# Batch 7's experts in the turned form, pair (1,0) second in the load queue, bias columns computed earlier

## The chip, the cores and the metric

The kernel runs on one core of one Trainium2 chip. The metric is the device time of one execution in microseconds, lower is better. A core has TensorE (matrix products, into PSUM banks), VectorE, ScalarE and GpSimd (elementwise work), SyncE (here it only issues transfers) and 16 DMA engines.

## The reference, cut to what matters

Eight batches of 128 rows by 128 channels, float32, pass through four residual layers. Layers 0 and 1 are mixed linear layers; the third is a mixture of experts with two chosen experts for each batch and one shared expert; the fourth picks one expert for each batch.

```python
# third layer (S=128, H=128, I=512, E=8, two experts of 8 for each batch)
w, sel = jax.lax.top_k(softmax(router_logits), 2)
w = w / w.sum(axis=-1, keepdims=True)
out  = sum over the two experts e of batch b:  w[b, e] * mlp(x[b], gate[e], up[e], down[e])
out += mlp(x, shared_gate, shared_up, shared_down)
# mlp(x, g, u, d) = (gelu(x @ g) * (x @ u)) @ d
# fourth layer (H=256, one expert of 8 for each batch)
up, gate = x @ W_up[e].T + b_up[e], x @ W_gate[e].T + b_gate[e]
out = (silu(up) * gate) @ W_down[e].T + b_down[e]
```

## The kernel before, in words

Everything is unrolled and ordered by hand: each engine has its own written list of steps, and semaphores tie them together. A step that waits holds up all that stands behind it on its engine.

**Stages.** Layers 0 and 1 are done by about 14 us. The shared expert follows, in eight steps `k` (four chunks of 128 for each half of the batches): TensorE forms gate and up in three wide products each (`shared_high`, `shared_middle`, `shared_low`; a float32 factor is split in a rounded part and a rest), ScalarE takes the gelu (L413) and rounds the hidden tile (`round_hidden`, L469), VectorE multiplies (`hidden`, L665), GpSimd subtracts the rounded part (`hidden_low_part`, L362), and `shared_down(k)` takes both. Then come the chosen experts, pair `(b, k)` being expert `k` of batch `b`, and layer 3 of batch `b` (called layer 3 in the code, the fourth of the reference) once both pairs are summed.

**Plain and turned batches.** In a plain batch (0 and 7) `gate_up` multiplies each 128-column chunk of a weight with x, in plain float32: 8 matmuls, 16 records of 128 columns in the trace. Its hidden tile has the hidden index on the partitions, and `down` (L935) reads it directly. In a turned batch (1 to 6) `gate_up_wide` makes x the stationary factor and streams 512 columns of weights: 3 products for gate and 3 for up (L918, L919, L921). For them ScalarE rounds both weights (`round_part`, L451, a ring of four in `wide_h`) and GpSimd forms the rests (`wide_low_part`, L357). The hidden tile comes out the other way round, so VectorE transposes it in 32 x 32 blocks (`turn`, L681) and SyncE swaps the blocks' places with four transfers of 128 KB (`swap`, L255), each 128 pieces of 1 KB; `down` then waits for `swapped`.

**Loads.** SyncE issues all of them, in an order written out: 16 pairs of 768 KB, 8 weights of layer 3 of 384 KB (`load_w3`), the swaps and the stores. There are 11 places for pairs, so the loads from (5,1) on wait until an earlier pair's down product is complete; those of (4,0) to (5,0) wait for the last `shared_down` (`down_done`, 8). `swap(b)` waits for both transposes of batch b and, from batch 3 on, for the down products of batch b - 2, whose tile it overwrites.

**Orders that matter here.** ScalarE, in the shared expert: gelu(k), round_hidden(k - 1), and from k = 4 one `round_part` of batch 1. SyncE: pairs (0,0), (0,1), (1,0), the weights of layer 3 of batch 0, (1,1), (2,0) and on. VectorE: the experts' selected biases (`bias_columns`: a product over 320 elements, a sum, a halving) between batch 1 and layer 3 of batch 0; ScalarE's `halve3` waits for them. `layer3(b)` on TensorE is four products into PSUM (L950), `down3(b)` its last two (L965).

Of the kernel before, what the change touches and what calls it, by code (L numbers as in the profile page):

```python
# [5 lines left out]
B, S, C = 8, 128, 128  # L6
E = 8
# [4 lines left out]
HC = H // 128  # L12
# [8 lines left out]
NSH = 2 * T  # L21
# [5 lines left out]
TURNED = range(1, B - 1)  # L27
# [9 lines left out]
def build(nc, x, head, rest_in, shared, skill, layer3, out):  # L37
# [8 lines left out]
    with ctx:  # L46
# [183 lines left out]
        with nc.Block() as block:  # L230

            @block.sync
            def _(sp):
# [37 lines left out]
                def pick(b, k):  # L271
                    picked[b, k] = expert(b, k)

                def load(b, k):
                    load_pair(b, k, picked[b, k])
# [3 lines left out]
                pick(0, 1)  # L279
                load(0, 1)  # L280
                pick(1, 0)
                load(1, 0)
                load_w3(0, picked[0, 0])
                for b, k in ((1, 1), (2, 0), (2, 1), (3, 0)):
                    pick(b, k)
                    load(b, k)
# [35 lines left out]
                for b in range(2, B - 2):  # L322
                    store(b, b % 2)
# [4 lines left out]
            def _(pool):  # L328
# [36 lines left out]
                for k in range(4):  # L365
                    hidden_low_part(k)
                wide_low_part(1, 0, 0)
                hidden_low_part(4)
                wide_low_part(1, 0, 1)
                hidden_low_part(5)  # L370
                wide_low_part(1, 1, 0)
                hidden_low_part(6)
                hidden_low_part(7)
                wide_low_part(1, 1, 1)
# [6 lines left out]
            def _(act):  # L381
# [90 lines left out]
                for k in range(1, NSH):  # L472
                    gelu_step(k, k % 2, shg_ps[k % 3])
                    round_hidden(k - 1)
                    if k >= 4:
                        round_part(1, (k - 4) // 2, (k - 4) % 2)
                round_hidden(NSH - 1)
                gelus(0)
# [13 lines left out]
                for b in range(5, B):  # L492
                    gelus(b)
                    if b == 5:
                        round_pair(6, 1)
                    halve3(b - 3)
                    tanh_step(b - 3)
                halve3(B - 3)
# [8 lines left out]
            def _(dve):  # L507
# [139 lines left out]

                def bias_columns():

                    n = 2 * HC + 1  # L650
                    then(dve.tensor_tensor(bias_hot[:, :, :, :], bias_t.unsqueeze(2).broadcast_to([128, n, B, E]),
                                           hot1[:, :, :].unsqueeze(1).broadcast_to([128, n, B, E]), ALU.mult))
                    then(dve.reduce_sum(bsel[:, :, :], bias_hot[:, :, :, :], axis=AX.X))
                    dve.tensor_scalar(half_bias[:, :, :], bsel[:, 0:HC, :], 0.5, None, ALU.mult).then_inc(bias_ready, 1)
# [96 lines left out]
                second_share()  # L751
                hidden(3, 1)
                share_sum()
                hidden(4, 0)
                share_scale()
                hidden(5, 1)
# [8 lines left out]
                add_shared(0)  # L765
                expert_hidden(1, 0)
                add_shared(1)
                residual(0)
                expert_hidden(1, 1)
                bias_columns()  # L770
# [29 lines left out]
            def _(pe):  # L800
# [214 lines left out]
                for b in range(5, B - 1):  # L1015
                    gate_up_wide(b, 0)
                    gate_up_wide(b, 1)
                    down3(b - 4, b % 2)
                    down(b - 2, 0)
                    down(b - 2, 1)  # L1020
                    layer3(b - 3)
                gate_up(B - 1, 0)
                gate_up(B - 1, 1)
                down3(B - 5, 1)
                down(B - 3, 0)
                down(B - 3, 1)
                layer3(B - 4)
                down(B - 2, 0)
                layer3(B - 3)
                down(B - 2, 1)  # L1030
                down3(B - 4, 0)
                down(B - 1, 0)
                down3(B - 3, 1)
                product3(B - 2, 0, 0, 0)
# [60 lines left out]
```

## Time and profile before

| | |
|---|---|
| median of 3 runs | 87.89 us (86.85 to 87.95) |
| the profiled execution, its own time | 86.78 us |
| its span, first to last instruction | 85.4 us |
| TensorE, matmuls | 78.1 us busy (91%) |
| VectorE; ScalarE; GpSimd | 52.3; 47.1; 46.0 us busy |
| transfers | 21.65 MB; the main queue 69.4% of 16 engines' span |
| granted TensorE clock | 1.0 throughout |

The busy times are averages over stages with different limits; the stages have to be read one by one. The span leaves out what lies before the first and behind the last instruction, 1.4 us of this execution.

### The profile page before, as it was taken

The page shows a single profiled execution, that of the slowest core. Times are in us where ns is not written, and L with a number is a line of the kernel's source. Part 1 is how long each engine was busy: PE and PEld are TensorE (multiplying, and loading weights), DVE is VectorE, ACT ScalarE, POOL GpSimd, SP SyncE. Part 2 cuts the span into 40 slices and gives each one's busy share as a digit, 9 for nine tenths or more (in the row PEclk, how much of TensorE's full clock was granted, in tenths as well). Part 3 has the DMA queues.
Part 4 walks back from the last instruction along what each step waited for, and adds up shares of the span by engine and source line. Part 5 has one row for each costly group of instructions (what it writes and reads, how often), then busy time and mean ns, then how long its engine had stood idle before and what let it go on. Part 6 is the DMA issues. An engine that isn't in the chain of part 4 may idle for free.

```text
span 85.4 us, 1612 instructions
## 1 busy us (share of the span) xinstructions
PE 78.1 (91%) x500; PEld 68.4 (80%) x500; DVE 52.3 (61%) x116; ACT 47.1 (55%) x95; POOL 46.0 (54%) x44
## 2 busy tenths in 40 slices
PE   6999899999994889999947999999999999999990
PEld 6979788888862778896825897988986999999990
DVE  1599399884003454449969983959645944456271
ACT  6500996864069859507489695572292072059270
POOL 3020567589129999999998999992092000000000
PEclk9999999999999999999999999999999999999999
DMA  1996000789999999389977999989999988600102
GB/s 15 380 373 239 3 0 0 236 348 365 405 397 423 426 407 394 125 282 374 421 203 140 345 376 291 321 222 319 352 402 396 370 247 189 222 0 8 37 24 61
DMA packets 8791, 21.65 MB, mean 253 GB/s; under 512 B 976, under 2 KB 5200, under 8 KB 8784
## 3 DMA queue, kind: packets, MB, share of 16 engines
q1 hardware_dynamic: 8496, 20.77, 69.4%
q10 hardware_dynamic: 288, 0.79, 2.4%
q8 instruction: 4, 0.07, 0.3%
q14 instruction: 3, 0.02, 0.1%
HBM read 17.88 MB, written 0.52 MB: 216 GB/s over the span
## 4 chain that ended last, share of the span: by engine, by line
PE 43%; DMA 27%; POOL 7%; DVE 7%; SPq 6%; ACT 4%; issue 4%; DVEq 0%
PE bank L935 15%; DMA pair_w<-in_skill 9%; DMA b_mix<-p 8%; PE bank L908 7%; DMA shared_sb<-in_shared 6%; PE bank L950 5%; PE bank L918 4%; PE bank L965 3%; PE bank L919 3%; PE bank L921 3%; POOL pair_low L357 3%; SPq L255 3%; POOL hid_l L362 3%; DMA head_sb<-in_head 3%; SPq L240 2%
## 5 line engine op out<-in xcount | busy, mean ns | idle before, releaser
L357 POOL TENSOR_TENSOR pair_low<-pair_w,wide_h 128x512 fp32r<-128x512 f32 x16 | 20.5, 1307 | 7.5 <-ACT wide_h L451 7.3
L413 ACT ACTIVATE gelu<-bank 128x512 f32<-128x512 f32 x24 | 14.0, 593 | 9.2 <-PE bank L921 6.5
L667 DVE SCALAR_TENSOR_TENSOR hid<-gelu,wsel,bank 128x512 f32<-128x512 f32 x16 | 11.8, 736 | 6.8 <-PE bank L935 2.2
L451 ACT ACTIVATE wide_h<-pair_w 128x512 fp32r<-128x512 f32 x16 | 9.3, 622 | 6.5 <-DMA pair_w<-in_skill 6.4
L918 PE MATMUL bank<-wide_h,x_h 128*128 128x512 f32 x24 | 10.0, 418 | 1.8 <-DVE hid L667 1.8
L362 POOL TENSOR_TENSOR hid_l<-hid,hid_h 128x512 fp32r<-128x512 f32 x8 | 10.2, 1288 | 1.9 <-ACT hid_h L469 1.9
L665 DVE TENSOR_TENSOR hid<-gelu,bank 128x512 f32<-128x512 f32 x8 | 5.5, 687 | 8.7 <-ACT gelu L413 4.4
L681 DVE STREAM_TRANSPOSE p<-hid 128x512 f32<-128x512 f32 x12 | 8.5, 712 | 1.7 <-DMA b_mix<-p 1.4
L919 PE MATMUL bank<-wide_h,x_l 128*128 128x512 f32 x24 | 9.4, 390 | 0.0
L423 ACT ACTIVATE half<-bank,half_bias 128x128 f32<-128x128 f32 x12 | 3.7, 361 | 10.0 <-PE bank L950 7.1
L908 PE MATMUL bank<-x_t,pair_w 128*128 128x128 f32 x64 | 7.8, 278 | 0.7 <-DVE hid L665 0.7
L908 PEld LDWEIGHTS bank<-x_t,pair_w 128*128 128x128 f32 x64 | 7.4, 192 | 1.2 <-DVE hid L665 1.2
L918 PEld LDWEIGHTS bank<-wide_h,x_h 128*128 128x128 f32 x24 | 4.5, 189 | 2.9 <-DVE hid L667 2.2
L712 DVE SCALAR_TENSOR_TENSOR gate<-bank,bsel,half 128x128 f32<-128x128 f32 x12 | 3.7, 346 | 5.1 <-ACT half L423 5.1
L950 PE MATMUL bank<-x_t,w 128*128 128x128 f32 x48 | 6.4, 277 | 0.2 <-DVE x_t L688 0.2
L921 PE MATMUL bank<-pair_low,x_h 128*128 128x512 f32 x16 | 6.4, 398 | 0.0
L341 POOL TENSOR_TENSOR shared_l<-shared_sb,shared_h 128x512 fp32r<-128x512 f32 x3 | 3.9, 1288 | 4.6 <-ACT shared_h L391 4.5
L950 PEld LDWEIGHTS bank<-x_t,w 128*128 128x128 f32 x48 | 5.8, 192 | 0.6 <-DVE x_t L688 0.6
L469 ACT ACTIVATE hid_h<-hid 128x512 fp32r<-128x512 f32 x8 | 5.0, 628 | 2.1 <-DVE hid L665 2.0
L871 PE MATMUL bank<-x_h,shared_h 128*128 128x512 f32 x16 | 5.8, 395 | 0.0
L879 PE MATMUL bank<-x_h,shared_l 128*128 128x512 f32 x16 | 5.8, 390 | 0.0
L919 PEld LDWEIGHTS bank<-wide_h,x_l 128*128 128x128 f32 x24 | 4.5, 189 | 0.7
(114 smaller groups left out, 157.1 us busy)
## 6 DMA issues: line engine op xcount, KB each, us to landing
pair_w<-in_skill SPq DMA_DIRECT2D x12, 768.0 KB, 8.0
w<-in_layer SPq DMA_DIRECT2D x6, 384.0 KB, 8.3
x_t<-p SPq DMA_DIRECT2D x12, 128.0 KB, 3.5
b_mix<-p SPq DMA_DIRECT2D x12, 128.0 KB, 4.0
shared_sb<-in_skill SPq DMA_DIRECT2D x1, 768.0 KB, 12.3
home_h<-in_skill SPq DMA_DIRECT2D x1, 768.0 KB, 4.6
home_l<-in_skill SPq DMA_DIRECT2D x1, 768.0 KB, 6.1
home_hid<-in_skill SPq DMA_DIRECT2D x1, 768.0 KB, 7.6
```

The lines of the kernel that those rows point to most:

```text
L357: pool.tensor_tensor(low_of(b, k)[:, m, :], w[:, m, :], wide_h[:, ring_at(b, k) % RING, m, :].bitcast(fp32), ALU.subtract).then_inc(wide_l ...
L362: pool.tensor_tensor(hid_l[:, k % 3, :], hid[:, k % 2, :], hid_h[:, k % 3, :].bitcast(fp32), ALU.subtract).then_inc(hid_low, 1)
L413: act.activation(gelu[:, n, :], ps[:, :], ACT.Gelu_apprx_tanh).then_inc(gelu_ready, 1)
L451: act.activation(wide_h[:, ring_at(b, k) % RING, m, :], w[:, m, :], ACT.Copy).then_inc(wide_high, 1)
L667: dve.scalar_tensor_tensor(hid[:, n, :], gelu[:, n, :], wsel[:, bass.DynSlice(weight, 1)], u_ps[n][:, :], ALU.mult, ALU.mult).then_inc(hid ...
L681: dve.transpose(turned[q][:, :, k, :], hid[:, k, :].rearrange("p (j s) -> p j s", j=T)).then_inc(turned_ready, 1)
L908: mm = pe.matmul(ps[:, S * t:S * (t + 1)], w[:, 1 + n, 128 * t:128 * (t + 1)], x2_t[:, columns(b)], start=True, stop=True)
L918: pe.matmul(ps[:, :], x2_h[:, S * b:S * (b + 1)], wide_h[:, n % RING, m, :], start=True, stop=False)
L919: pe.matmul(ps[:, :], x2_l[:, S * b:S * (b + 1)], wide_h[:, n % RING, m, :], start=False, stop=False)
L921: pe.matmul(ps[:, :], x2_h[:, S * b:S * (b + 1)], low_of(b, k)[:, m, :], start=False, stop=True).then_inc(done, 1)
L935: mm = pe.matmul(acc_ps(b)[:, 0:S].rearrange("p (a s) -> p a s", s=QUAD), w[:, part, C * t:C * (t + 1)], by_chunk[:, t, :, :], start=(k == ...
L950: pe.matmul(ps[:, S * c:S * (c + 1)], w[:, n, 128 * c:128 * (c + 1)], x3_t[:, b % 4, :], start=True, stop=True).then_inc(done, 1)
```

## The change

Batch 7 joins the turned batches (`TURNED`). With it come its four roundings on ScalarE (the pair (7,0) after batch 5's layer-3 step, (7,1) after batch 6's gelus), four subtractions on GpSimd, two transposes on VectorE, and `swap(7)` on SyncE, for which `store(2, 0)` is moved ahead. On TensorE the order of the end is changed: both down steps of batch 6 come before layer 3 of batch 5, and the first product of batch 6's layer 3 comes ahead of batch 7's first down step.

At the start, SyncE loads (1,0) second, then (0,1), (1,1), and only then the first weights of layer 3. ScalarE rounds (1,0) one step k later, and (1,1) between the two gelus of batch 0; GpSimd's subtractions follow that order. The bias columns are split in three steps, spread between the shared expert's hidden products on VectorE, and the second add of the shared sum comes ahead of the product of (1,0).

```diff
--- before.py
+++ after.py
@@ -24,7 +24,7 @@
 PAIRS, THIRD = 7, 3
 RING = 4
 IN_BANK = 4
-TURNED = range(1, B - 1)
+TURNED = range(1, B)
 
 
 HEAD = 2 * C + B + B * E
@@ -276,12 +276,11 @@
 
                 pick(0, 0)
                 load(0, 0)
-                pick(0, 1)
-                load(0, 1)
-                pick(1, 0)
-                load(1, 0)
+                for b, k in ((1, 0), (0, 1), (1, 1)):
+                    pick(b, k)
+                    load(b, k)
                 load_w3(0, picked[0, 0])
-                for b, k in ((1, 1), (2, 0), (2, 1), (3, 0)):
+                for b, k in ((2, 0), (2, 1), (3, 0)):
                     pick(b, k)
                     load(b, k)
                 pick(3, 1)
@@ -319,7 +318,9 @@
                 store(1, 1)
                 swap(6)
                 load_w3(7, picked[7, 0], 3)
-                for b in range(2, B - 2):
+                store(2, 0)
+                swap(7)
+                for b in range(3, B - 2):
                     store(b, b % 2)
                 store(B - 2, 0)
                 store(B - 1, 1)
@@ -362,15 +363,14 @@
                     pool.tensor_tensor(hid_l[:, k % 3, :], hid[:, k % 2, :], hid_h[:, k % 3, :].bitcast(fp32),
                                        ALU.subtract).then_inc(hid_low, 1)
 
-                for k in range(4):
+                for k in range(5):
                     hidden_low_part(k)
                 wide_low_part(1, 0, 0)
-                hidden_low_part(4)
+                hidden_low_part(5)
                 wide_low_part(1, 0, 1)
-                hidden_low_part(5)
-                wide_low_part(1, 1, 0)
                 hidden_low_part(6)
                 hidden_low_part(7)
+                wide_low_part(1, 1, 0)
                 wide_low_part(1, 1, 1)
                 for b in TURNED[1:]:
                     for k in range(TOP_K):
@@ -472,10 +472,12 @@
                 for k in range(1, NSH):
                     gelu_step(k, k % 2, shg_ps[k % 3])
                     round_hidden(k - 1)
-                    if k >= 4:
-                        round_part(1, (k - 4) // 2, (k - 4) % 2)
+                    if k in (5, 6):
+                        round_part(1, 0, k - 5)
                 round_hidden(NSH - 1)
-                gelus(0)
+                gelu_step(NSH, 0, g_ps[0])
+                round_pair(1, 1)
+                gelu_step(NSH + 1, 1, g_ps[1])
                 round_batch(2)
                 gelus(1)
                 round_batch(3)
@@ -491,10 +493,12 @@
                 tanh_step(1)
                 for b in range(5, B):
                     gelus(b)
-                    if b == 5:
-                        round_pair(6, 1)
+                    if b < B - 1:
+                        round_pair(b + 1, 1)
                     halve3(b - 3)
                     tanh_step(b - 3)
+                    if b == 5:
+                        round_pair(7, 0)
                 halve3(B - 3)
                 tanh_step(B - 3)
                 act.preload_act_table(ACT.Silu)
@@ -645,12 +649,17 @@
                     mark(dve.scalar_tensor_tensor(wsel[:, :].rearrange("p (b k) -> p b k", k=TOP_K), wnorm[:, :, :],
                                                   STOP_SCALE, wpart[:, :, :], ALU.mult, ALU.add))
 
+                def bias_pick():
+                    n = 2 * HC + 1
+                    mark(dve.tensor_tensor(bias_hot[:, :, :, :], bias_t.unsqueeze(2).broadcast_to([128, n, B, E]),
+                                           hot1[:, :, :].unsqueeze(1).broadcast_to([128, n, B, E]), ALU.mult))
+
                 def bias_columns():
-
-                    n = 2 * HC + 1
-                    then(dve.tensor_tensor(bias_hot[:, :, :, :], bias_t.unsqueeze(2).broadcast_to([128, n, B, E]),
-                                           hot1[:, :, :].unsqueeze(1).broadcast_to([128, n, B, E]), ALU.mult))
-                    then(dve.reduce_sum(bsel[:, :, :], bias_hot[:, :, :, :], axis=AX.X))
+                    settled()
+                    mark(dve.reduce_sum(bsel[:, :, :], bias_hot[:, :, :, :], axis=AX.X))
+
+                def bias_halves():
+                    settled()
                     dve.tensor_scalar(half_bias[:, :, :], bsel[:, 0:HC, :], 0.5, None, ALU.mult).then_inc(bias_ready, 1)
 
                 def hidden(k, n, weight=None):
@@ -749,10 +758,13 @@
                 first_share()
                 hidden(2, 0)
                 second_share()
+                bias_pick()
                 hidden(3, 1)
                 share_sum()
+                bias_columns()
                 hidden(4, 0)
                 share_scale()
+                bias_halves()
                 hidden(5, 1)
                 norm_shares()
                 hidden(6, 0)
@@ -763,11 +775,10 @@
                 expert_hidden(0, 0)
                 expert_hidden(0, 1)
                 add_shared(0)
+                add_shared(1)
                 expert_hidden(1, 0)
-                add_shared(1)
                 residual(0)
                 expert_hidden(1, 1)
-                bias_columns()
                 layer3(0)
                 expert_hidden(2, 0)
                 expert_hidden(2, 1)
@@ -1012,26 +1023,20 @@
                 down(2, 0)
                 down(2, 1)
                 layer3(1)
-                for b in range(5, B - 1):
+                for b in range(5, B):
                     gate_up_wide(b, 0)
                     gate_up_wide(b, 1)
                     down3(b - 4, b % 2)
                     down(b - 2, 0)
                     down(b - 2, 1)
                     layer3(b - 3)
-                gate_up(B - 1, 0)
-                gate_up(B - 1, 1)
-                down3(B - 5, 1)
-                down(B - 3, 0)
-                down(B - 3, 1)
-                layer3(B - 4)
                 down(B - 2, 0)
+                down(B - 2, 1)
                 layer3(B - 3)
-                down(B - 2, 1)
                 down3(B - 4, 0)
+                product3(B - 2, 0, 0, 0)
                 down(B - 1, 0)
                 down3(B - 3, 1)
-                product3(B - 2, 0, 0, 0)
                 down(B - 1, 1)
                 pe.wait_ge(silu3_ready, 1)
                 product3(B - 2, 0, 0, 1)
```

## Rows read from the trace of the kernel before

**Rows 1.** Chain of work that ended last, shares of the span by engine
```profile
PE 43%; DMA 27%; POOL 7%; DVE 7%; SPq 6%; ACT 4%; issue 4%; DVEq 0%
```

**Rows 2.** Timeline, ScalarE: start, length, instruction, count, [idle before <-releaser]
```profile
19.62 0.62 ACT L469 ACTIVATE hid_h<-hid 128x512 fp32r<-128x512 f32 x1
...
24.34 0.63 ACT L451 ACTIVATE wide_h<-pair_w 128x512 fp32r<-128x512 f32 x1 [4.09 <-DMA pair_w<-in_skill]
```

**Rows 3.** Loads by time of issue (15.3; 16.4): size, us to landing
```profile
pair_w<-in_skill SPq DMA_DIRECT2D x1, 768.0 KB, 7.1
...
pair_w<-in_skill SPq DMA_DIRECT2D x1, 768.0 KB, 7.9
```

**Rows 4.** Timeline of GpSimd
```profile
25.05 1.28 POOL L357 TENSOR_TENSOR pair_low<-pair_w,wide_h 128x512 fp32r<-128x512 f32 x1 [3.44 <-ACT wide_h L451]
...
33.68 9.21 POOL L357 TENSOR_TENSOR pair_low<-pair_w,wide_h 128x512 fp32r<-128x512 f32 x7
...
62.02 2.54 POOL L357 TENSOR_TENSOR pair_low<-pair_w,wide_h 128x512 fp32r<-128x512 f32 x2 [3.89 <-ACT wide_h L451]
```

**Rows 5.** Timeline of TensorE, first half
```profile
20.74 0.62 PE L887 MATMUL bank<-x_l,shared_h 128*128 128x512 f32 x2
...
34.86 0.39 PE L918 MATMUL bank<-wide_h,x_h 128*128 128x512 f32 x1
...
36.22 1.95 PE L935 MATMUL bank<-hid,pair_w 128*128 128x128 f32 x16
...
45.46 0.50 PE L918 MATMUL bank<-wide_h,x_h 128*128 128x512 f32 x1 [1.79 <-DVE hid L667]
```

**Rows 6.** Timeline of VectorE around the bias columns
```profile
41.05 0.69 DVE L651 TENSOR_TENSOR bias_hot<-rest_sb,hot 128x320 f32<-128x320 f32 x1
...
42.30 0.63 DVE L654 TENSOR_SCALAR half_bias<-bsel 128x16 f32<-128x16 f32 x1
...
44.67 0.74 DVE L667 SCALAR_TENSOR_TENSOR hid<-gelu,wsel,bank 128x512 f32<-128x512 f32 x1
```

**Rows 7.** Stretches: engines' busy time, granted clock, DMA share, GB/s
```profile
34.00:37.00 3.00, 3.00 (x19) 2.60 (x17) 1.21 (x2) 1.37 (x3) 3.00 (x3) 1.00 0.51 137
43.00:46.00 3.00, 1.21 (x5) 0.69 (x5) 2.25 (x5) 2.97 (x8) 2.76 (x3) 1.00 0.64 154
47.50:54.40 6.90, 6.90 (x44) 5.92 (x43) 5.12 (x10) 5.02 (x10) 6.90 (x7) 1.00 0.99 342
```

**Rows 8.** VectorE's wait; loads issued 54.4, 55.6, 59.5; batch 4's swap, 58.0
```profile
65.74 0.71 DVE L681 STREAM_TRANSPOSE p<-hid 128x512 f32<-128x512 f32 x1 [0.95 <-DMA b_mix<-p]
...
pair_w<-in_skill SPq DMA_DIRECT2D x1, 768.0 KB, 6.9
...
pair_w<-in_skill SPq DMA_DIRECT2D x1, 768.0 KB, 8.6
...
pair_w<-in_skill SPq DMA_DIRECT2D x1, 768.0 KB, 8.1
...
b_mix<-p SPq DMA_DIRECT2D x2, 128.0 KB, 6.5
```

**Rows 9.** The end: TensorE, VectorE, SyncE; landing of batch 6's swap
```profile
68.47 3.74 PE L908 MATMUL bank<-x_t,pair_w 128*128 128x128 f32 x32
72.05 0.61 PE L965 MATMUL bank<-hid,late_w 128*128 128x128 f32 x4
...
76.07 1.06 PE L950 MATMUL bank<-x_t,w 128*128 128x128 f32 x8
...
79.64 0.39 PE L950 MATMUL bank<-x_t,w 128*128 128x128 f32 x2
...
78.05 0.29 DVE L688 TENSOR_TENSOR x_t<-bank,x2s 128x128 f32<-128x128 f32 x1
...
67.86 3.03 SPq L255 DMA_DIRECT2D b_mix<-p  x4
...
b_mix<-p SPq DMA_DIRECT2D x1, 128.0 KB, 3.0
```


## The prediction

> **What bounds the kernel now.** I read the chain that ended last first [rows 1]: TensorE (PE) holds 43% of it and transfers 27%, so two things are nearly full at once. The timelines then say where. PE works back to back from 45.5 us on, and its idle time lies before that, behind one late transfer. ScalarE finishes a rounding at 20.25 us and next has the rounding of the first turned pair, (1,0), in its order; that pair lands at 24.3, so the engine stands still for 4.09 us with five gelus and roundings of the shared layer queued behind [rows 2]. The load table shows why: the pair is third in SyncE's queue. The second transfer, issued at 15.3 and 7.1 us on its way, lands at 22.4; the third, issued at 16.4, takes 7.9 and lands at 24.3 [rows 3]. GpSimd (POOL) idles 3.44 us, from 21.6 to 25.05 [rows 4], and then runs on without a pause: 25.05 to 33.68 is seven subtractions, 1.23 us each. PE reaches the first wide products at 34.86 instead of running through [rows 5]. A second stall is at 45.46, 1.79 us, released by the hidden product of VectorE (DVE) for pair (2,0); that product stands behind the bias columns, 41.05 to 42.93, and behind layer 3 of batch 0 [rows 5, 6].
>
> The other resource is the DMA engines. From 47.5 to 54.4 they are busy for 0.99 of the time; only two gaps of size are left after 30 us: 34 to 37 at a share of 0.51 (1.5 us idle) and 43 to 46 at 0.64 (1.1 us idle) [rows 7]. Where PE waits in the second half, it waits for these or comes just behind them: DVE's transpose of (6,0) waits 0.95 us for the swap of batch 4, which lands at 65.7 [rows 8], and POOL idles 3.89 us before the low parts of pair (6,1), whose load took 6.9 us from 54.4 and landed at 61.3 [rows 4, 8].
>
> **First part: the queue at the start.** Pair (1,0) takes the second place and lands near 22.4 instead of 24.3; (0,1) lands at 24.3, and PE wants it near 27.9, so it costs nothing. The rounding of (1,0) also moves behind the next gelu. ACT is free at 20.25; PE's fifth shared product is complete about 21.1 (its last two products start at 20.74 [rows 5]), so the gelu runs 21.2 to 21.8, the rounding of that hidden tile to 22.4, and POOL starts its next subtraction at 22.4. From there to the low part of (1,1), second half, stand eight subtractions: 22.4 + 8 x 1.23 = 32.3, against 33.68 + 1.23 = 34.9 before [rows 4]. PE: from 20.74 there are 2 + 3 + 6 + 3 + 6 + 3 = 23 wide matmuls of 0.228 each (six of them from 34.86 to 36.22 [rows 5]), 5.2 us, then batch 0's plain products, 2 x 1.79, then nine more of 0.228, 2.05: 20.74 + 5.2 + 3.6 + 2.05 = 31.6. I find no wait in between that outlasts this (the last low part of the shared layer is there at 29.9). So (1,0) starts at about 31.7 rather than 34.86: **PE is 3.1 us ahead.**
>
> **Second part: bias columns.** Three DVE instructions leave 41.05 to 42.93 (1.9 us). Their new places lie among the shared hidden products, where DVE waits for gelus and low parts anyway; 0.65, 0.5 and 0.6 us delay three hidden products by 0.3 to 0.6, all of which wait for POOL or ScalarE anyway. Without that cover they would cost at most the same 1.9 us. At the far end: PE could be at pair (3,0) at 31.7 + 1.37 + 1.79 + 1.37 + 0.9 + 2.74 = 39.9. ACT has gelu (1,1) done at 36.5, then four roundings of 0.57, two halves, a tanh: 39.8; DVE gates by 40.4 and forms (2,0) by 41.2. So a stall of 1.3 us stays of the 1.79, and (3,0) starts at 41.2 instead of 45.46: 4.2 us ahead. The second add of the shared sum only trades places with one hidden product, into time where DVE waits for PE's down product; nothing.
>
> A row and a rule on the bias steps: the last of them writes 16 elements a partition and yet takes 0.63 us, ending at 42.93 [rows 6], just as POOL's long group ends at 42.89 [rows 4]. The Trainium skill, page "SBUF — State Buffer", section "SBUF: two separate sides", says that VectorE and GpSimd share a port pair as an exclusive lock held for the whole instruction; the trace agrees in this instruction. By that rule each of the three could be held for a whole subtraction in its new place, and the final gain would be some 0.4 us smaller than my sum. The sum itself takes the rows as they are.
>
> **How much of 4.2 us survives the DMA engines.** They do the same work as before, in nearly the same order, so what they deliver can only come earlier by the idle time that is filled. The loads of batch 4 may go when the shared sum is complete, at 31.8 instead of some 35 [rows 5], which is before the queue runs dry: the gap at 34 to 37 closes, 1.5 us. The next loads stand behind the swap of batch 1, which follows PE's lead of 3 us, so the gap at 43 to 46 closes, 1.1 us. Sum 2.6, and small idle shares elsewhere may add up to 0.4 (a guess). PE was touching the DMA already, so its lead falls to **3.0 us** by batch 6 (2.6 to 3.4): pair (6,1) lands at 58.3 instead of 61.3, the swap of batch 4 near 62.7.
>
> **Third part: batch 7 turned.** Removed: 32 matmul records from 68.47 to 72.05, 3.58 us [rows 9]. Added: 12 wide matmuls of 0.228, 2.74. PE gains **0.84 us**. Beside it: ACT gets four roundings of 0.57 (2.3 us, in a stretch where it has six instructions of its own); POOL four subtractions (5.0 us) where it has ended; DVE two transposes of 0.71 [rows 8]. Are they in time? Pair (7,1) was issued at 59.5 and took 8.1 us, so it landed at 67.6, and the plain products wanted it at 70.3 [rows 8, 9]. Now 64.6, and two roundings of 0.6 and two subtractions come after it; the second subtraction starts 1.25 behind the first: 64.6 + 0.6 + 2 x 1.25 = 67.7. PE, 3.0 ahead, comes to that matmul at 68.0. No stall, 0.3 to spare. The rounding of (7,0) stands in ACT's order ahead of batch 6's gelus; issued at 55.6 and 8.6 us on its way [rows 8], that pair landed at 64.2 and will at 61.2. That delays a gelu by some 2 us and the swap of batch 6 by 1, to 71.2, when PE wants it at 71.3.
>
> **Fourth part: the swap and the end.** Before, DVE's hidden product went straight to PE. Now four more transfers of 128 KB follow, on SyncE behind the swap of batch 6, the last weights and a store, and they also wait for the down product (5,1). PE: wide products of batch 7 end at 68.2, then 0.45 + 1.79 = 70.45. SyncE issues four in 2.6 us or so (3.03 us for batch 6's four), each 3.0 us to land [rows 9]: issue of the last 72.4, landing 75.4. PE meanwhile has layer 3 of batch 4, down (6), layer 3 of batch 5 and a layer-3 down, 0.9 + 1.79 + 0.9 + 0.45 (records of 128 columns follow each other at 3.58 / 32 = 0.112 us; these steps have 8, 16, 8 and 4), and stands at 74.5 before the first product of batch 6's layer 3. That one now stands ahead of down (7,0) and needs the residual of batch 6. The same steps before: layer 3 of batch 5 starts at 76.07, the residual ends at 78.34, 2.27 later [rows 9]. Now 73.15 + 2.3 = 75.5. So PE stalls **1.0 us**, and the swap is hidden under the same stall. Bounds: 0 if both are quicker, 2.5 if SyncE or the landing is 1.5 us slower. From there to the end: before 85.4 - 79.64 = 5.76 with this product in it, now one down step (0.9) and one layer-3 down (0.45) more: 75.5 + 7.1 = 82.6.
>
> **Sum**, against the profiled execution: -3.0 (lead) - 0.84 + 1.0 = -2.8. Span 85.4 to 82.6, its time 86.78 to 84.0. The three runs have a median 1.1 us above that execution and one of them is with it, so I put the new median halfway, at 84.5. About 2% (1.8 us) is what a measurement here tells from nothing.
>
> **Rivals.**
> 1. The DMA engines do not limit (chance 0.2). PE keeps 4.2 ahead: -4.2 - 0.84 + 1.0 = -4.0, profiled 82.8. For it: the packets of swaps keep the engines busy at a low rate, and could run quicker if spread. Against: 0.99 busy for seven us.
> 2. The head start is smaller (0.2). Pair (1,0) lands later than 22.4, or the bias steps hold up the shared layer by one subtraction or more, or ACT's early wait for (7,0) pushes batch 6's swap: lead 2.0, stall 1.2, -1.6, profiled 85.1.
> 3. The start does nothing (0.06): (1,0) still lands at 24.3, or the loads of the next pairs slide by as much. Only the 0.84 and the stall are left: -0.8 to +0.3; profiled 86.5.
> 4. Slower (0.04). One mechanism, the swap of batch 7. From its landing to the end stand down (7,0), a layer-3 down, down (7,1) and 4.65: 6.9 us. It makes the kernel no faster from a landing at 78.5, and slower by 2% from one at 80.2. If its transfers need 6.5 us, as those of batch 4 did behind queued loads [rows 8], and no lead was made (issue from 73.5), it lands at 82.0 and the span is 88.9, +3.5. Against: after 74 us the queue is nearly empty.
> My forecast has 0.5. Range of the median: 83.0 (rival 1, low base) to 86.4 (rival 2, high base). Faster by over 2%: 0.5 + 0.2 + half of rival 2 = 0.79; slower 0.04; the rest 0.17.
>
> **What would show it.** ACT's wait at L451 near 20 us gone or under 0.3 us, POOL continuous from 22.4; first L918 matmul near 31.7; the stall before pair (3,0) about 1.3 us; DMA share over 0.9 throughout 34 to 46; PE waiting for swaps or for low parts between 49 and 62 us, where its lead shrinks from 4 to 3; wide products for batch 7 without a stall; one PE stall of about 1 us at L950 before the last down products, with DVE's L688 as the releaser. The prediction is wrong if PE stays 4 ahead past 60 us, if a stall over 1.5 us stands at the last L935 with a DMA as the releaser, or if the DMA gaps stay open.

## The result, and the profile after

The changed kernel takes 83.47 us (median of 4, 83.01 to 84.70) against 87.37 us (86.62 to 87.95) before: ratio 0.956, 95% interval 0.942 to 0.970, faster. Two later measurements of the same kernel gave 83.73 us each (against 87.30 and 87.31), ratios 0.957 (0.951 to 0.964) and 0.976 (0.968 to 0.983). Every ratio in this document compares only the executions within 1.5% of the fastest of their kernel, so it can differ from the quotient of the medians, which are of all executions. Forecast: 84.5, range 83.0 to 86.4.

The profile taken with the result is of the slowest execution, 84.70 us with a span of 83.0; so where a time matters I also show the last of the later profiles (83.48 us, span 81.9), called the quicker profile below. First the one with the result. ScalarE (ACT), TensorE (PE), GpSimd (POOL), VectorE (DVE) and SyncE, timelines, engine by engine (start, length, instruction, idle time before it and what ended it):

```profile
22.19 0.62 ACT L469 ACTIVATE hid_h<-hid 128x512 fp32r<-128x512 f32 x1
22.71 0.62 ACT L451 ACTIVATE wide_h<-pair_w 128x512 fp32r<-128x512 f32 x1
...
32.11 0.39 PE L929 MATMUL bank<-wide_h,x_h 128*128 128x512 f32 x1
...
41.21 0.50 PE L929 MATMUL bank<-wide_h,x_h 128*128 128x512 f32 x1 [0.79 <-DVE hid L676]
...
51.43 2.05 PE L946 MATMUL bank<-b_mix,pair_w 128*128 128x128 f32 x16 [1.97 <-DMA b_mix<-p]
...
75.83 0.49 PE L961 MATMUL bank<-x_t,w 128*128 128x128 f32 x2 [0.71 <-DVE x_t L697]
...
22.89 1.29 POOL L363 TENSOR_TENSOR hid_l<-hid,hid_h 128x512 fp32r<-128x512 f32 x1 [0.75 <-ACT hid_h L469]
...
21.62 0.55 DVE L663 TENSOR_SCALAR half_bias<-bsel 128x16 f32<-128x16 f32 x1
...
71.18 2.50 SPq L255 DMA_DIRECT2D x_t<-p  x4
```

Batch 7's swap, its last transfer, size and us to landing:

```profile
x_t<-p SPq DMA_DIRECT2D x1, 128.0 KB, 2.8
```

The two stretches in which transfers had idled (the last three columns are granted clock, DMA share and GB/s):

```profile
34.00:37.00 3.00, 3.00 (x23) 2.75 (x22) 1.75 (x4) 0.85 (x2) 3.00 (x4) 1.00 1.02 390
43.00:46.00 3.00, 3.00 (x21) 2.44 (x21) 2.33 (x5) 1.95 (x4) 3.00 (x3) 1.00 0.96 292
```

What is to be seen: the wait of 4.09 us [rows 2] is gone; ACT rounds pair (1,0) with no idle time before it. PE reaches the wide products at 32.1 instead of 34.86 [rows 5], pair (3,0) at 41.2 instead of 45.46. Both DMA gaps [rows 7] are closed, 0.51 to 1.02 and 0.64 to 0.96. And there is a stall that was not there: 1.97 us before down (2,0), released by batch 2's swap. The last stall, 0.71, is the one before batch 6's first layer-3 product.

The three stalls of PE after 28 us in the quicker profile of the changed kernel:

```profile
40.70 0.50 PE L929 MATMUL bank<-wide_h,x_h 128*128 128x512 f32 x1 [0.79 <-DVE hid L676]
...
50.30 2.05 PE L946 MATMUL bank<-b_mix,pair_w 128*128 128x128 f32 x16 [1.36 <-DMA b_mix<-p]
...
74.70 0.49 PE L961 MATMUL bank<-x_t,w 128*128 128x128 f32 x2 [0.71 <-DVE x_t L697]
```

The lead of PE over the kernel before, read from the starts of the same steps in the two timelines (before, and the quicker profile):

| step | before | changed | lead, us |
|---|---|---|---|
| first wide product | 34.86 | 31.60 | 3.26 |
| pair (3,0) | 45.46 | 40.70 | 4.76 |
| down (2,0), behind the stall of 1.36 | 53.36 | 50.30 | 3.06 |
| first product of batch 7 | 68.47 | 64.75 | 3.72 |
| layer-3 down behind batch 7's products | 72.05 | 67.57 | 4.48 |
| last group of matmuls | 82.32 | 78.82 | 3.50 |

The lead grows by 0.66 between 53 and 68 us because two short waits of the kernel before are gone (a low part of pair (6,1) at 64.62, batch 4's swap at 65.69), by 0.76 through batch 7's wide products, and loses 0.98 at the last stall (0.71 idle, the rest its restart). The span is 85.4 - 81.9 = 3.5 shorter.

### The profile page after: what moved, and what is told of

Same layout as the page of the kernel before. It is cut to its first block, busy times and chain, and to the rows that moved or that the text cites. A ratio compares the mean times of both kernels' runs of the same rounds, so it can differ in the third digit from the quotient of the medians.

```text
span 83.0 us, 1591 instructions
## 1 busy us (share of the span) xinstructions
PE 76.8 (93%) x480; PEld 68.1 (82%) x480; DVE 54.2 (65%) x118; ACT 49.4 (59%) x99; POOL 50.7 (61%) x48
## 4 chain that ended last, share of the span: by engine, by line
PE 82%; DMA 7%; DVE 4%; SPq 2%; issue 2%; ACT 1%; DVEq 0%; ACTq 0%
PE bank L946 15%; PE bank L961 8%; DMA b_mix<-p 7%; PE bank L929 6%; PE bank L932 6%; PE bank L930 6%; PE bank L882 4%; PE bank L898 4%; PE bank L890 4%; PE bank L919 4%; PE bank L821 4%; PE bank L813 3%; PE bank L976 3%; SPq L255 2%; PE bank L906 2%; PE bank L908 2%
## 5 line engine op out<-in xcount | busy, mean ns | idle before, releaser
L358 POOL TENSOR_TENSOR pair_low<-pair_w,wide_h 128x512 fp32r<-128x512 f32 x20 | 25.2, 1293 | 4.3 <-ACT wide_h L451 4.3
L451 ACT ACTIVATE wide_h<-pair_w 128x512 fp32r<-128x512 f32 x20 | 11.5, 623 | 4.0 <-DMA pair_w<-in_skill 4.0
L929 PE MATMUL bank<-wide_h,x_h 128*128 128x512 f32 x28 | 11.7, 416 | 0.8 <-DVE hid L676 0.8
L690 DVE STREAM_TRANSPOSE p<-hid 128x512 f32<-128x512 f32 x14 | 10.0, 712 | 2.0 <-DMA b_mix<-p 1.0
L930 PE MATMUL bank<-wide_h,x_l 128*128 128x512 f32 x28 | 10.9, 391 | 0.0
L932 PE MATMUL bank<-pair_low,x_h 128*128 128x512 f32 x20 | 7.8, 390 | 0.0
L929 PEld LDWEIGHTS bank<-wide_h,x_h 128*128 128x128 f32 x28 | 5.3, 189 | 2.0 <-DVE hid L676 1.2
L946 PE MATMUL bank<-x_t,pair_w 128*128 128x128 f32 x48 | 6.3, 277 | 0.0
L946 PEld LDWEIGHTS bank<-x_t,pair_w 128*128 128x128 f32 x48 | 5.8, 192 | 0.4 <-DMA x_t<-p 0.4
L946 PE MATMUL bank<-b_mix,pair_w 128*128 128x128 f32 x32 | 4.0, 278 | 2.0 <-DMA b_mix<-p 2.0
```

The lines of the kernel that those rows point to most:

```text
L358: pool.tensor_tensor(low_of(b, k)[:, m, :], w[:, m, :], wide_h[:, ring_at(b, k) % RING, m, :].bitcast(fp32), ALU.subtract).then_inc(wide_l ...
L451: act.activation(wide_h[:, ring_at(b, k) % RING, m, :], w[:, m, :], ACT.Copy).then_inc(wide_high, 1)
L690: dve.transpose(turned[q][:, :, k, :], hid[:, k, :].rearrange("p (j s) -> p j s", j=T)).then_inc(turned_ready, 1)
L929: pe.matmul(ps[:, :], x2_h[:, S * b:S * (b + 1)], wide_h[:, n % RING, m, :], start=True, stop=False)
L930: pe.matmul(ps[:, :], x2_l[:, S * b:S * (b + 1)], wide_h[:, n % RING, m, :], start=False, stop=False)
L932: pe.matmul(ps[:, :], x2_h[:, S * b:S * (b + 1)], low_of(b, k)[:, m, :], start=False, stop=True).then_inc(done, 1)
```

## The experiments

Each is told against the kernel before, run beside it on the same chip. Three chips were used, four kernels on each; the medians of before were 86.51, 87.30 and 87.31 us.

### The change in parts

**Start only.** The kernel before with the load queue and the new order of roundings and subtractions:

```diff
-                pick(0, 1)
-                load(0, 1)
-                pick(1, 0)
-                load(1, 0)
+                for b, k in ((1, 0), (0, 1), (1, 1)):
+                    pick(b, k)
+                    load(b, k)
                 load_w3(0, picked[0, 0])
...
-                    if k >= 4:
-                        round_part(1, (k - 4) // 2, (k - 4) % 2)
+                    if k in (5, 6):
+                        round_part(1, 0, k - 5)
```

> The kernel before with only the start changed: pair (1,0) second in the load queue and the roundings and subtractions of batch 1 in their new order; bias columns stay between batches 1 and 2, batch 7 stays plain. Theory (the DMA engines cap the lead): PE reaches the first wide products about 3 us earlier, keeps about 2.2 at pair (3,0) because the bias columns still stand in the way there, and ends 1.9 to 2.4 us faster than before. Rival (no cap, PE's own stalls decide): the full 3.0 us, and the DMA share between 34 and 46 us stays well under 0.9.

Measured: 88.82 us (88.19 to 89.34, 4 runs), ratio 1.040 (1.021 to 1.060). Neither theory: **slower than before**, each of its four executions above all seven of before (85.00 to 87.82). The timelines of this kernel, DVE, then POOL, then PE:

```profile
38.08 4.84 DVE L651 TENSOR_TENSOR bias_hot<-rest_sb,hot 128x320 f32<-128x320 f32 x1
42.95 0.49 DVE L653 TENSOR_REDUCE bsel<-bias_hot 128x40 f32<-128x320 f32 x1
43.48 0.17 DVE L654 TENSOR_SCALAR half_bias<-bsel 128x16 f32<-128x16 f32 x1
...
30.10 10.02 POOL L356 TENSOR_TENSOR pair_low<-pair_w,wide_h 128x512 fp32r<-128x512 f32 x8
40.09 2.48 POOL L356 TENSOR_TENSOR shared_low<-shared_sb,wide_h 128x512 fp32r<-128x512 f32 x2
46.32 2.52 POOL L356 TENSOR_TENSOR shared_h<-home_h,wide_h 128x512 fp32r<-128x512 f32 x2 [3.75 <-ACT wide_h L449]
...
46.19 0.79 PE L918 MATMUL bank<-wide_h,x_h 128*128 128x512 f32 x1 [5.53 <-DVE hid L667]
```

Its stretches around the stall:

```profile
40.00:45.00 5.00, 0.66 (x3) 0.19 (x2) 4.19 (x5) 1.28 (x4) 2.57 (x3) 0.87 0.92 264
46.00:50.00 4.00, 3.81 (x11) 3.24 (x12) 2.93 (x5) 2.40 (x5) 3.68 (x3) 0.50 0.44 159
```

The product of the bias columns, 0.69 us before [rows 6], took 4.84 us. It ends at 42.92, and POOL's unbroken run, whose last ten subtractions the first two lines show, ends at 42.57: the product got through only when POOL had nothing left to do. Behind it waits ACT's `halve3`, behind that DVE's hidden product, and PE stood idle for 5.53 us. The granted clock fell from 1.00 to 0.50 (the 1.2 GHz level) between 43 and 44 us, in the middle of that stall, and was full again from 51 us. So the stretch from pair (3,0) to down (1,0) took 51.51 - 46.19 = 5.3 us where the changed kernel needs 44.12 - 40.70 = 3.4: another 1.9 us.

**Bias columns only.**

```diff
                 second_share()
+                bias_pick()
                 hidden(3, 1)
                 share_sum()
+                bias_columns()
                 hidden(4, 0)
                 share_scale()
+                bias_halves()
```

> The kernel before with only the bias columns moved among the shared hidden products (and the second shared add ahead of pair (1,0)). Theory: the stall of 1.79 us before pair (3,0) falls to under 1 us, the DMA gap at 43 to 46 us closes partly while that at 34 to 37 stays; 0.8 to 1.4 us faster. Rival (the three bias steps are held by GpSimd's port lock and slow the shared layer): the first wide product later than 34.9, gain under 0.4 us.

Measured: 86.86 us against 86.51, ratio 1.018 (0.996 to 1.039): no difference that can be told, and my theory's 0.8 to 1.4 us are not there. The rival had the time right and its cause wrong: the first wide product starts at 34.47, not later than 34.9, and the three bias steps take 0.48, 0.49 and 0.55 us in their new places. PE in its profile:

```profile
43.57 0.50 PE L925 MATMUL bank<-wide_h,x_h 128*128 128x512 f32 x1 [0.80 <-DVE hid L672]
53.17 2.05 PE L942 MATMUL bank<-b_mix,pair_w 128*128 128x128 f32 x16 [1.55 <-DMA b_mix<-p]
```

The stall at pair (3,0) fell to 0.80 as expected, and PE was 1.9 us ahead there. All but 0.2 us of it was gone at down (2,0), behind a wait of 1.55 us for batch 2's swap: batch 4's loads had been issued only 0.4 us earlier than before (34.83 against 35.22), and the DMA share from 34 to 37 us was still 0.56.

**Batch 7 only.**

```diff
-TURNED = range(1, B - 1)
+TURNED = range(1, B)
```

with `swap(7)` and the new orders of the end.

> The kernel before with only batch 7 turned and the end's order rearranged. Theory: 0.84 us fewer matmul time, and a stall of 0.7 to 1.0 us before the first layer-3 product of batch 6 (released by VectorE's residual): within 0.4 us of before. Rival (the stall is covered and the turn pays in full): 0.8 us faster; other rival (the swap of batch 7 comes last): 1 us or more slower, with a DMA as the releaser.

Measured: 87.05 us (86.10 to 87.89) against 86.51 (85.00 to 87.82): 0.5 us apart where the theory had at most 0.4, and with such a spread neither rival is excluded by the medians. The stall stands where it was expected, 0.72 us at the first layer-3 product of batch 6, released by DVE's residual.

**Start and bias together, batch 7 plain.**

> Both changes at the start, batch 7 plain and the old end. Theory: the whole gain of the change is here: 3.0 to 3.9 us faster than before, within 0.4 us of the changed kernel. Rival (batch 7 gives its 0.84 us): 2.4 to 3.1 us faster. If start and bias simply add, this equals the sum of the two single runs; if the DMA engines cap the lead it is less than that sum.

Measured: 83.26 us (82.75 to 84.69) against 86.51, ratio 0.973 (0.959 to 0.988). The medians differ by 3.3 us, the ratio stands for 2.3: all that can be told of the gain is here. The parts do not add: alone they gave +2.3 and +0.3.

**The same again, beside the changed kernel** on one chip, six executions each:

> Start and bias, batch 7 plain, on the same chip as the changed kernel. Theory (batch 7's 0.84 us is given back in the stall of 0.71 us before the first layer-3 product of batch 6, released by the residual): equal to the changed kernel within 0.4 us. Rival (the turn pays): 0.5 to 0.9 us slower than it.

> The changed kernel once more, the measure for the others on this chip: 83.0 to 84.0 us.

Measured: 83.48 us with batch 7 plain (five executions from 82.12 to 84.04, one at 88.87 with a granted clock of 0.857), 83.73 us for the changed kernel (83.38 to 84.61). Turning batch 7 gains nothing that can be measured, as the theory said.

### Why the bias steps stood still

The Trainium skill, page "SBUF — State Buffer", section "SBUF: two separate sides", says that VectorE and GpSimd share a port pair as an exclusive lock: of a GpSimd instruction and a VectorE instruction that has two SBUF inputs (when the GpSimd one reads SBUF) or runs in a 2-port performance mode, the one that starts first holds it for its whole length and the other waits. Two more kernels ask whether it is GpSimd's run that holds the bias steps.

**The product moved early, sum and halving in the old place** (start-only kernel otherwise):

```diff
                 second_share()
+                bias_pick()
                 hidden(3, 1)
```

> The start-only kernel (88.8 us) with one of the three bias instructions moved early: the product over 320 elements, which reads two SBUF tensors and took 4.84 us there beside GpSimd's back-to-back subtractions. Sum and halving stay where they were. Theory A (the product waits for a free moment of the port that VectorE shares with GpSimd): it takes 0.5 us in its new place, the 5.5 us stall of TensorE before pair (3,0) falls to 2 us or less, the granted clock stays at 1.0 and the kernel comes to 83.5 to 85.5 us. Rival B (any bias step in the old place is late, or the stall comes from elsewhere): 88 us or more.

Measured: four executions at 86.86, 83.54, 86.89 and 86.88 us; before on that chip 87.30. Between the two theories. DVE in the profile (86.86 us):

```profile
36.98 0.44 DVE L655 TENSOR_REDUCE bsel<-bias_hot 128x40 f32<-128x320 f32 x1
37.46 4.06 DVE L656 TENSOR_SCALAR half_bias<-bsel 128x16 f32<-128x16 f32 x1
```

The block has moved to the halving: 16 elements a partition, 4.06 us, where the start-only kernel shows 0.17 once POOL was idle. The sum before it is not held, 0.44. So a small size does not protect an instruction. One execution of the four was 3.3 us quicker and had the full clock; whether its halving got through I can't say, as it has no trace. Theory A erred in taking the product for the only one that can be shut out. PE's stall before pair (3,0) was 4.47 us in this profile.

**GpSimd made to wait.** The start-only kernel, every bias step in its old place, and one wait added:

```diff
                 for b in TURNED[1:]:
+                    if b == 3:
+                        pool.wait_ge(bias_ready, 1)
```

> The start-only kernel (88.8 us) with one wait more and nothing else: GpSimd does not begin the subtractions of batch 3 before the three bias steps, in their old place, are through. Theory A (VectorE's bias steps are shut out of SBUF as long as GpSimd's subtractions follow each other without a gap): the product falls from 4.84 us to under 1.6, the halving is short, TensorE's stall of 5.5 us before pair (3,0) falls to 1.5 to 3 us, the granted clock stays at full, and the kernel comes to 83.5 to 85.5 us although a wait was added. Rival B (the bias steps are slow for another reason): still 88 us or more.

Measured: **82.62 us** (81.83 to 83.41) against 87.31, ratio 0.961 (0.948 to 0.974). A wait on an engine that was busy without a pause took 6.2 us off the start-only kernel's 88.82 (across chips; the medians of before differ by 0.8). DVE, POOL and PE:

```profile
37.17 0.45 DVE L653 TENSOR_TENSOR bias_hot<-rest_sb,hot 128x320 f32<-128x320 f32 x1
37.65 0.49 DVE L655 TENSOR_REDUCE bsel<-bias_hot 128x40 f32<-128x320 f32 x1
38.17 0.17 DVE L656 TENSOR_SCALAR half_bias<-bsel 128x16 f32<-128x16 f32 x1
...
38.43 2.53 POOL L356 TENSOR_TENSOR pair_low<-pair_w,wide_h 128x512 fp32r<-128x512 f32 x2 [1.70 <-DVE half_bias L656]
...
40.88 0.50 PE L920 MATMUL bank<-wide_h,x_h 128*128 128x512 f32 x1 [1.10 <-DVE hid L669]
```

4.84 us became 0.45, POOL lost 1.70 us that nobody missed, PE's stall fell from 5.53 to 1.10, and the granted clock is 1.0. This shows the cause: against the start-only kernel nothing was changed but POOL's activity beside the bias steps. That the lock on the port pair is what holds them is the account of the Trainium skill; the runs show only that GpSimd's unbroken run does. The median is also 1.1 us below that of the changed kernel on the same chip, with neither the bias columns moved nor batch 7 turned; the intervals of the ratios overlap, and part of it is a start of the first load at 13.4 us in this profile against 14.0 in the changed kernel's, which no edit accounts for. So the pause does what the move of the bias columns was for: the gain needs the bias steps out of GpSimd's way, by either edit.

### Are the DMA engines the cap?

**Lighter loads.** The changed kernel, but the five loads from (5,1) on bring two of their three parts; the down products of those pairs use the weights already lying there.

```diff
+                    if TOP_K * b + k >= len(homes):
+                        sp.dma_start(w[:, 0:2, :], skill[..., part:part + 2, :]...).then_inc(landed, 16)
+                        return
```

> The changed kernel, but the five loads from pair (5,1) on move only the first two of their three parts (512 instead of 768 KB); their down products use the weights already lying there, so that part of the result is another batch's. Theory (the DMA engines cap the lead that the start makes): TensorE's stall of 1.97 us before down (2,0) falls below 0.8 us and the kernel is 1.0 to 2.0 us faster than the changed one. Rival (the swap is late by its own issue and latency): no change within 0.4 us.

Measured: 82.51 us against 83.73 for the changed kernel on that chip (before: 87.30), ratio to before 0.943 (0.935 to 0.950). It leaves out a third of five loads, so its result is not the reference's. PE's stall before down (2,0) is gone altogether; its three stalls after 28 us:

```profile
41.06 0.50 PE L932 MATMUL bank<-wide_h,x_h 128*128 128x512 f32 x1 [0.79 <-DVE hid L679]
60.70 0.50 PE L935 MATMUL bank<-pair_low,x_h 128*128 128x512 f32 x1 [0.17 <-POOL pair_low L361]
74.07 0.49 PE L964 MATMUL bank<-x_t,w 128*128 128x128 f32 x2 [0.71 <-DVE x_t L700]
```

1.2 us faster with 1.3 MB less in all, 0.5 MB of it ahead of the swap: the amount of transfers sets that stall, as the theory said.

**The swap ahead of one load.**

```diff
-                load(6, 0)
                 swap(2)
+                load(6, 0)
```

> The changed kernel with swap(2) issued ahead of load (6,0). Theory (transfers are served in the order of issue, and the swap stands behind two loads of 2 us each): the swap lands about 1.9 us earlier, the stall before down (2,0) goes, pair (6,0) lands after 51 us, where it is not yet needed; 0.5 to 1.8 us faster than the changed kernel. Rival (the total of the transfers is what counts): the wait moves to pair (6,1) or swap(4), and the end is within 0.4 us of the changed kernel.

Measured: 84.72 us (84.02 to 85.08) against 83.73 (83.44 to 84.10) for the changed kernel: about 1 us slower, where one theory had 0.5 to 1.8 faster and the rival no change. In its profile the wait before down (2,0) is indeed gone. PE from there on:

```profile
48.93 1.95 PE L946 MATMUL bank<-b_mix,pair_w 128*128 128x128 f32 x16
...
54.64 0.71 PE L976 MATMUL bank<-hid,w 128*128 128x128 f32 x4
...
60.71 0.50 PE L932 MATMUL bank<-pair_low,x_h 128*128 128x512 f32 x1
...
61.74 1.16 PE L946 MATMUL bank<-b_mix,home_h 128*128 128x128 f32 x8
...
64.44 0.47 PE L929 MATMUL bank<-wide_h,x_h 128*128 128x512 f32 x1
```

Down (2,0) is 1.37 us earlier than in the quicker profile of the changed kernel (50.30), the first product of batch 7 only 0.31 (64.44 against 64.75). The difference went into three waits of the weight loads: 0.56 us at 54.6 (ACT's halves stood behind the rounding of the late pair (6,0)), 0.57 at 60.7 for the low part of pair (6,1), 0.28 at 61.7 for batch 4's swap. The last two are those that the rival named. The span is 81.6 us, no longer than the changed kernel's; the other executions have 83.0 to 83.5. What makes those longer is in no trace. Settled is that the order is no gain, and in the profile why: the wait moved.

**The changed kernel again**, for these two:

> The changed kernel itself, on the chip of these runs: 83.0 to 84.0 us, the measure for the other three.

Measured: 83.73 us; stalls 0.80, 1.15 and 0.71 us in the same three places.

### The end

**Old order of layer 3 of batch 5, and the swap issued by two engines.**

```diff
                 down(B - 2, 0)
-                down(B - 2, 1)
                 layer3(B - 3)
+                down(B - 2, 1)
...
+                        act.wait_ge(down_done, down_at(b - 2, 1))
+                        for a in range(T // 2, T):
+                            act.dma_start(hid_t[1][:, a, :, :], turned[1][...]).then_inc(swapped[1], 16)
                     halve3(b - 3)
```

> The changed kernel with layer 3 of batch 5 back between the two down steps of batch 6, and the last two of swap(7)'s four transfers issued by ScalarE instead of SyncE. Theory: the residual of batch 6 is there in time and the swap lands about 1.2 us earlier, so the 0.71 us stall goes: 0.4 to 0.8 us faster than the changed kernel. Rival (the swap's landing was hidden just behind that stall and is not made shorter by two issuers): within 0.2 us, with a DMA as the releaser at the last down products.

Measured: 83.97 us (83.17 to 84.97) against 83.73: no gain. ACT and PE:

```profile
70.18 1.57 ACTq L502 DMA_DIRECT2D x_t<-p  x2
71.94 0.63 ACT L423 ACTIVATE half<-bank,half_bias 128x128 f32<-128x128 f32 x2 [4.12 <-PE bank L951]
...
72.70 1.26 PE L966 MATMUL bank<-x_t,w 128*128 128x128 f32 x8 [0.83 <-ACT half L423]
```

The two issues kept ACT for 1.57 us, its halves of batch 4 came late, and PE waited 0.83 us for them at layer 3 of batch 5: the stall moved one step forward. Neither of my two outcomes named that wait. The run changes two things at once, the order and the issuer; what the order alone would do stays open.

## Why the prediction was right, point by point

The time (84.5, measured 83.47), the sign and the range were right. So were most terms of the sum, read in the quicker profile of the changed kernel:

- **The head start.** Forecast 3.1 us at the first wide product; measured 3.26, and 2.75 in the first profile, which issued its first load 0.4 us later than before. POOL's chain starts at 22.38, forecast 22.4.
- **Pair (3,0).** Forecast 4.2 us ahead with a stall of 1.3; measured 4.8 and 0.79. Here ACT's halves followed the roundings at once.
- **The cap.** Forecast: the lead falls to 3.0 us (2.6 to 3.4) because only the two DMA gaps can be filled. Measured 3.06 behind the wait for batch 2's swap; that the amount of transfers sets this wait is shown by the light loads. I had placed the loss at "batch 6". The good agreement is in part luck of the profile. Seven profiles have this load order with the bias steps out of the way; by the time of their first load (13.40, 14.02, 14.16, 14.28, 14.48, 14.55, 14.66; before 14.18) they begin down (2,0) at 48.99, 50.30, 50.26, 50.28, 50.45, 51.43 and 51.85, so their lead there is 4.4, 3.1, 3.1, 3.1, 2.9, 1.9 and 1.5 us. The first, the kernel with GpSimd's wait, has no wait there and its span is 5.0 us shorter than before. The cap is no fixed 3 us: it moves with the start of the loads, which differs from execution to execution and which my sum took as given.
- **Batch 7.** 0.76 less, forecast 0.84; 0.98 given back at the stall (0.71 of it idle), forecast 1.0; the net of about zero is shown by the run with batch 7 plain. Swap(7) took 2.50 us to issue and 2.8 to land, forecast 2.6 and 3.0.
- **The sum.** Forecast -3.0 - 0.84 + 1.0 = -2.8 of span; by the quicker profile -3.06 - 0.66 - 0.76 + 0.98 = -3.5, by the first one -2.4. The 0.66 is the wait for the low part of pair (6,1) and that for batch 4's swap. I had read both rows [rows 4, 8] and left them out of the sum; they are nearly the whole of its error.
- **The base.** I put the median half a microsecond above the time of the profiled execution, halfway up to the spread of three runs. The measured medians lie 1.0 and 0.8 us under my 84.5, near the low end of the range. The shares in the last line of the rivals are mis-added by 0.01: 0.5 + 0.2 + 0.1 is 0.80.

**Where the reasoning was wrong, without harm to the number,** is the second part, the bias columns. I priced their move by the rows of the trace of before (1.9 us in the *old* place, of which 1.1 us of lead come back, 3.1 to 4.2), as if those lengths would stay when the start moved by 3 us. They do not: there the product takes 4.84 us, and without its move the start alone is slower than before by 2.3 us. I had the row that betrayed it, a halving of 16 elements at 0.63 us, but I applied the port lock only to the *new* places and priced it at 0.4 us. In the new places there was next to nothing to pay: 0.48, 0.49 and 0.55 us. I also said that each of the three could be held; the sum never was (0.44 to 0.49 us). The move of three short instructions is what makes the other edit pay. My sum came out because both were in the change; had I been asked about the start alone, I would have forecast the wrong sign, as my expectation of that run did.

## What to carry to other kernels

When an edit shifts work in time, go through every short VectorE instruction that will now lie beside an unbroken run of GpSimd work: its time in the old trace says nothing of its time there. A short wait that opens a gap in that run can be worth more than any reordering. And where the DMA engines are at 0.9 or more, add up their idle time first: here 2.6 us of gaps went with a lead of about 3 us that lasted out of 4.8, give or take the start of the first load.

## What the runs showed of the hardware

- GpSimd's back-to-back subtractions can shut a VectorE instruction out for several of them in a row (4.84 us for a product of two SBUF tensors, 4.06 us for a float32 halving from SBUF to SBUF), not only until the one under way has ended. It need not be so: a product of 16 elements a partition took 0.26 us in the kernel before, and in the changed kernel, where it began 0.04 us behind a subtraction of 1.29 us, it took 1.28 us and was through with that one.

```profile
26.09 0.26 DVE L636 TENSOR_TENSOR wnorm<-pk,rpksum 128x16 f32<-128x16 f32 x1
...
22.89 1.29 POOL L363 TENSOR_TENSOR hid_l<-hid,hid_h 128x512 fp32r<-128x512 f32 x1 [0.75 <-ACT hid_h L469]
...
22.93 1.28 DVE L640 TENSOR_TENSOR wnorm<-pk,rpksum 128x16 f32<-128x16 f32 x1
```

- In the kernel before, the bias product was let in after some 0.25 us (0.69 us in all [rows 6], against 0.45 where POOL pauses), and one of POOL's subtractions there lasted 1.55 us where the others took about 1.3. That run was not quite unbroken: POOL had stood for some 0.15 us at 40 us. Whether this matters no run shows; what decides who gets in next stays open.
- A sum (0.44 to 0.49 us) and hidden products with one PSUM operand (0.70 to 0.75) were never held. For the product the rule of the Trainium skill's page named above agrees with the trace. For the halving it would need the 2-port mode, which no run here shows. That the wait can span several of GpSimd's instructions the page does not state.
- In the start-only profile PE idled for 5.53 us, and the granted clock was 0.50 from about 44 to 50.5 us, at a price of 1.9 us. But the length of one wait does not tell: the batch-7-only profile has 1.00 through a stall of 1.80 us at 45 us, and 0.50 from about 28 to 31 us, behind waits of 0.35, 0.85 and 0.33 us between 24.6 and 27.4. There batch 0's plain products took 5.22 us to the next step, in the changed kernel 3.49. The profile of the kernel before has waits of 0.59, 0.85 and 0.32 us at that place and the full clock, so what decides is open. The first row is the fall, the second lies in the low stretch:

```profile
27.00:28.00 1.00, 0.67 (x5) 0.65 (x5) 0.74 (x2) 1.00 (x3) 1.00 (x2) 0.87 0.98 406
29.00:30.00 1.00, 1.00 (x7) 1.00 (x7) 0.93 (x2) 0.21 (x1) 1.00 (x1) 0.50 1.08 442
```

- Of the 25 executions of before beside the experiments, 14 had a mean granted clock of 0.98 and 11 the full clock; all 14 of the changed kernel had 1.0, and its start has none of those early waits. On the last chip the 7 with 0.98 took 85.82 to 87.77 us and the 4 with the full clock 85.68 to 86.67; on the second chip the two with the full clock (87.23 and 87.30) were no quicker than the median of before. So of the gain against the median of before a part, up to 1.1 us on one chip and none on another, may be the clock. That the missing waits keep it up is likely and not shown.
